# Dense edge counts for the first 512 nodes of a graph network, and how its one-hots are built

## What is computed

```python
def _sage_layer(x, src, dst, inv_deg, W_self, W_neigh, b):
    agg = jax.ops.segment_sum(x[src], dst, num_segments=N_NODES)
    mean = agg * inv_deg[:, None]
    return x @ W_self + mean @ W_neigh + b
...
x = x + gnn(layernorm(x))          # three such layers, relu between them
x = x + ffn(layernorm(x))          # gelu(x w1 + b1) w2 + b2 for the selected nodes, scaled by the weight
```

## Time and profile before

| | us |
|---|---|
| time before, median of 3 runs | 6282.49 (6279.57 to 6283.19) |
| the profiled execution | 6277.99 |
| its span | 6276.2 |
| gathers of layer 0 | 145.8 to 2101.0 |
| gathers of layer 1 | 2136.5 to 4091.8 |
| gathers of layer 2 | 4110.9 to 6089.5 |

### The profile page before, as it was taken

One profiled execution on the slowest core, in us unless ns is written; L12 is line 12 of the kernel. 1 busy time (PEld: TensorE's weight loads), 2 busy tenths in 40 slices (PEclk: granted clock), 3 DMA queues, 4 the chain that ended last, 5 costly groups with the idle time before them and its releaser, 6 DMA issues.

```text
span 6276.2 us, 96211 instructions
## 1 busy us (share of the span) xinstructions
PE 4104.0 (65%) x20011; PEld 2433.3 (39%) x20012; DVE 2259.7 (36%) x4900; ACT 946.2 (15%) x2227; POOL 4448.2 (71%) x4700
## 2 busy tenths in 40 slices
PE   0445656677778645555666676654566788899993
PEld 0222333344445322222223333322234556677772
DVE  7112223333444311122223334421223344555556
ACT  6000000111111100000000000100011223334440
POOL 0777777777777577777777777767777777777750
PEclk9677778888999866677777788866778899999996
DMA  7555555565666555555556666655555656666644
GB/s 246 158 158 160 163 165 166 168 170 170 173 174 175 148 158 158 163 164 165 167 168 170 171 173 175 176 147 159 161 164 165 168 170 170 175 175 176 178 136 167
DMA packets 459717, 1053.84 MB, mean 168 GB/s; under 512 B 127891, under 2 KB 234087, under 8 KB 459687
## 3 DMA queue, kind: packets, MB, share of 16 engines
q0 software_dynamic: 300288, 922.79, 52.5%
q10 hardware_dynamic: 82908, 97.60, 4.5%
q1 hardware_dynamic: 76491, 33.10, 2.0%
HBM read 969.11 MB, written 84.02 MB: 168 GB/s over the span
## 4 chain that ended last, share of the span: by engine, by line
POOL 47%; issue 19%; PE 19%; DMA 11%; DVE 2%; ACT 1%; POOLq 1%; DVEq 0%; SPq 0%; ACTq 0%
POOL gath L494 47%; DMA gath<-table,idx_ring 10%; PE agg L609 8%; PE agg L611 3%; PE y L664 2%; PE hid L654 2%; PE y L548 1%; DMA idx_ring<-idx_dram 1%; PE hid L548 0%; PE hid L611 0%; PE lo L611 0%; PE hid L573 0%; DMA resid<-x 0%; POOLq L490 0%; PE tp L535 0%
## 5 line engine op out<-in xcount | busy, mean ns | idle before, releaser
L494 POOL DMA_INDIRECT gath<-table,idx_ring x4692 | 4447.4, 948 | 1641.5 <-issue 1539.4
L609 PE MATMUL agg<-gath,onehot 128*128 x5856 | 2464.8, 450 | 2007.9 <-SPq L429 1815.4
L609 PEld LDWEIGHTS agg<-gath,onehot 128*128 x5856 | 633.7, 108 | 3086.4 <-issue 2776.8
L883 DVE TENSOR_TENSOR onehot<-ids_ps,dst_f 128x512 f32 x1464 | 1012.8, 692 | 1980.3 <-PE agg L611 1126.5
L611 PE MATMUL agg<-gath,onehot 128*128 x3904 | 1238.2, 317 | 0.0
L611 PEld LDWEIGHTS agg<-gath,onehot 128*128 x3904 | 424.1, 109 | 127.8
L914 DVE SCALAR_TENSOR_TENSOR resid<-agg,inv_deg,resid 128x256 f32 (+1 forms) x196 | 94.7, 483 | 863.8 <-PE agg L611 863.1
L664 PE MATMUL y<-w_sb,hidT 128*128 128x256 f32 x1568 | 378.0, 397 | 3.0 <-ACT hidT L1244 3.0
L654 PEld LDWEIGHTS hid<-featT,w_gnn 128*128 128x128 f32 x3136 | 365.9, 192 | 4.9
L654 PE MATMUL hid<-featT,w_gnn 128*128 128x128 f32 x3136 | 366.5, 275 | 0.0
L1131 ACT ACTIVATE featT<-tp 128x256 f32<-128x256 f32 x196 | 75.0, 383 | 1886.3 <-PE tp L535 1769.3
(11 more groups left out here) (136 smaller groups left out, 2750.8 us busy)
## 6 DMA issues: line engine op xcount, KB each, us to landing
gath<-table,idx_ring POOLq DMA_INDIRECT x4692
table<-split ACTq DMA_DIRECT2D x194, 192.0 KB
table<-gath ACTq DMA_DIRECT2D x24, 768.0 KB, 3.6
xb<-x ACTq DMA_DIRECT2D x97, 128.0 KB
yw_dram<-yw ACTq DMA_DIRECT2D x97, 128.0 KB, 2.9
resid<-x SPq DMA_DIRECT2D x24, 512.0 KB, 7.8
gath<-yw_dram SPq DMA_DIRECT2D x24, 512.0 KB, 8.8
out<-gath ACTq DMA_DIRECT2D x24, 512.0 KB, 9.0
```

The costliest lines, as they stand in the source:

```text
L494: g.indirect_dma_start(gath[:, j, 0:PARTS * D], None, table[layer][:, :], bass.IndirectOffsetOnAxis(ap=idx_ring[:, h, i:i + 1], axis=0)).t ...
L609: mm(agg[p][:, 0:2 * D], oh, tile_rows[:, :, 0:2 * D], start=False, **flags)
L883: v.tensor_tensor(onehot[:, bass.ds(pair, GROUP), :], window_ids[p].unsqueeze(1).to_broadcast([P, GROUP, P]), dst_f[:, bass.ds(tiles, GROU ...
```

## The change

Nodes 0 to 511 (windows 0 to 3, `DENSE`) get their sums in layers 1 and 2 from a dense matrix of edge counts, not from gathers.

- In layer 0, slots 6 to 69, the counts are built. 128 groups of four nodes, two in a slot: for each edge tile of a group VectorE writes a one-hot of the source's low seven bits (128 columns) and one of four nodes times 100 source chunks (400 columns); TensorE multiplies them into the bank `count_ps`; ScalarE copies the 400 columns to `stage`, and stores them to DRAM each eight groups. Ahead of it, in slot 4, the sources are split and the groups' tile borders are counted.
- In layers 1 and 2 the windows come in the order 4 to 34, then 0 to 3, then 35 to 97 (`window_of`). In slots 6 to 30 TensorE multiplies a block of counts (1 MB) with 512 rows of the layer's f32 features (512 KB), four chunks by four windows, and sums into two PSUM banks; ScalarE issues both loads a slot ahead. In slots 31 to 34 nothing is gathered.
- GpSimd and SyncE start both layers at the turn of window 4's first block (`t0`, counted in turns).
- ScalarE also copies each product in f32 (`y32`) and stores it for the dense part. `w2` is loaded after layer 0, since its buffer serves the counts.
- `RING` is 16 tiles, four blocks, and the index ring is halved with it. Half of the output's buffers lie in the new buffer `dense`.
- `ids_ps` is gone. In layer 1 the window's ids lie in `count_ps` and one operation writes a block's one-hots as before; in layers 0 and 2 four operations do, one for each tile, each adding the window's base to `iota_row` and comparing with the tile's destinations.

The core of the diff:

```diff
-RING = 32
+RING = 16
...
+DENSE = 4
+CHUNKS_PER_BLOCK = 4
+GROUP_NODES = 4
+COUNT_COLS = 100
+DENSE_AT = 6
+COUNT_AT = 6
+COUNT_RING = 4
...
+        y32 = [sb(f"y32_{p}", [P, D]) for p in range(2)]
+        group_tiles = sb("group_tiles", [1, COUNT_GROUPS + 1], I32)
+        skipped = sb("skipped", [1, 2], I32)
...
-        ids_ps = psum("ids_ps", [P, 512])
-        window_ids = [ids_ps[:, p * P:(p + 1) * P] for p in range(2)]
...
+        count_ps = psum("count_ps", [P, 512])
+        dense_banks = [None, (lo0[:], hid[:, 1, :]), (lo0[:], count_ps[:])]
+        dense_ps = [banks and [t[:, h * D:(h + 1) * D] for t in banks for h in range(2)] for banks in dense_banks]
+        window_ids = [count_ps[:, p * P:(p + 1) * P] for p in range(2)]
...
+        def window_of(layer, n, part):
+
+
+            if layer == 0 or not exists(n):
+                return n
+            if isinstance(n, int):
+                if n < DENSE_WINDOWS:
+                    return n + DENSE
+                return n - DENSE_WINDOWS if n < DENSE_WINDOWS + DENSE else n
+            return n + DENSE if part[0] == 0 else n
...
-            sp.dma_start(w2_sb[:], w2.rearrange("(k p) n -> p k n", p=P)).then_inc(w_loaded, 16)
...
+            sp.dma_start(src_low.bitcast(I32), idx_dram[:, 0:PADDED]).then_inc(src_loaded, 16)
...
+            pool.wait_ge(steps_ready, 1)
+            t0, turns_left = first_block(pool)
...
+                with pool.Fori(t0 if layer else 0, FULL_TURNS) as it:
...
+            def count_group(g):
+
+                lo, hi = pe_groups(g)
+                pe.wait_ge(count_copied, g + 2)
+                flags = dict(start=False, skip_group_check=True)
+                mm(count_ps[:, 0:1], zeros[:], ones_bf[:, 0:1], start=True, stop=False, skip_group_check=True)
+
+                def count_tile(t, stop):
+                    slot = pe.snap((t + g) % COUNT_RING)
+                    pe.wait_ge(count_hots, t + g + 1)
+                    return mm(count_ps[:, 0:GROUP_NODES * COUNT_COLS], low_hots[:, bass.ds(slot, 1), :],
+                              key_hots[:, bass.ds(slot, 1), :], stop=stop, **flags)
+                with pe.If(lo < hi):
+                    with pe.Fori(lo, hi) as t:
+                        count_tile(t, False).then_inc(count_used, 1)
+                count_tile(hi, True).then_inc(count_ready, 1)
...
+                for c in range(2 if last_block else CHUNKS_PER_BLOCK):
+                    r = TAIL_ROWS if last_block and c == 1 else P
+                    for w in range(DENSE):
+                        ends = last_block and c == 1
+                        last = mm(dense_ps[layer][w], counts[p][0:r, w * P:(w + 1) * P, c], node_rows[p][0:r, c, :],
+                                  start=False, stop=ends, skip_group_check=True)
+                last.then_inc(dense_done, 1)
...
+                w = window_of(layer, n, part)
+                if not gathered(layer, w):
+                    pe.wait_ge(dense_done, layer * DENSE_BLOCKS)
+                    pe.wait_ge(agg_ready, layer * NT + n)
+                    pe.sem_inc(agg_ready, 1)
+                    return
+                first, shared = pe_blocks(half_of(layer, half, part, w), p)
+                if layer and isinstance(n, int) and n == 0:
+                    first = pe.snap(pe_t0 * RING_BLOCKS)
...
+                if part and part[0] == 0:
+                    for j in range(2):
+                        count_group(part[1] * 8 + (part[2] * 2 + j))
...
+                dense_step(1, w, p, part)
...
+            RING_BITS = RING_BLOCKS.bit_length() - 1
+            v.tensor_scalar(skipped[0:1, 0:1], win_block[0:1, DENSE // 2, 0:1], RING_BITS, None,
...
-                    dve.wait_ge(slots_free, b + (layer * PADDED_BLOCKS + 2))
-                    v.tensor_tensor(onehot[:, bass.ds(pair, GROUP), :],
-                                    window_ids[p].unsqueeze(1).to_broadcast([P, GROUP, P]),
-                                    dst_f[:, bass.ds(tiles, GROUP)].unsqueeze(2).to_broadcast([P, GROUP, P]),
-                                    ALU.is_equal).then_inc(onehot_ready, 1)
+                    dve.wait_ge(slots_free, b + dve_base[layer])
+                    if layer == 1:
+                        v.tensor_tensor(onehot[:, bass.ds(pair, GROUP), :],
+                                        window_ids[p].unsqueeze(1).to_broadcast([P, GROUP, P]),
+                                        dst_f[:, bass.ds(tiles, GROUP)].unsqueeze(2).to_broadcast([P, GROUP, P]),
+                                        ALU.is_equal).then_inc(onehot_ready, 1)
+                        return
+                    dve.sem_inc(dve_turn, 1)
+                    for j in range(GROUP):
+                        last = v.tensor_scalar(onehot[:, bass.ds(pair, GROUP), :][:, j, :], iota_row[:],
+                                               window_base[:, col(w)], dst_f[:, bass.ds(tiles, GROUP)][:, j:j + 1],
+                                               ALU.add, ALU.is_equal)
+                    last.then_inc(onehot_ready, 1)
...
+                    o = feat[p] if layer < 2 else rest
+                    dve.sem_inc(half_added, 1)
+                    if layer == 1:
+                        dve.wait_ge(tp_ready, turned(2, n - 2))
+                    v.scalar_tensor_tensor(out=o[0:r, :], in0=dense_ps[layer][w][0:r, :], scalar=inv, in1=total,
+                                           op0=ALU.mult, op1=ALU.add
+                                           ).then_inc(feat_ready if layer < 2 else o_ready, 1)
+                    return
...
+            def count_onehots(g):
+
+                lo, hi = dve_groups(g)
+                dve.wait_ge(count_copied, g + 1)
+                dve.sem_inc(dve_turn, 1)
+                with dve.Fori(lo, hi + 1) as t:
+                    slot = dve.snap((t + g) % COUNT_RING)
+                    dve.wait_ge(count_used, t + 2)
+                    dve.sem_inc(dve_turn, 1)
+                    v.tensor_scalar(low_hots[:, bass.ds(slot, 1), :], iota_row[:].unsqueeze(1),
+                                    src_low[:, bass.ds(t, 1)], None, ALU.is_equal)
+                    v.tensor_scalar(key_hots[:, bass.ds(slot, 1), :], iota_keys.unsqueeze(1),
+                                    group_base[:, col(g)], src_key[:, bass.ds(t, 1)],
+                                    ALU.add, ALU.is_equal).then_inc(count_hots, 1)
...
+                y = product_ps(phase, p)[0:r, 0:D]
+                a.copy(y32[p][0:r, :], y)
+                a.copy(split[p][0:r, 0, :], y).then_inc(hi_ready, 1)
                 act.wait_ge(rest_ready, upto(phase, n))
+                act.wait_ge(hi_ready, upto(phase, n))
+                act.dma_start(window_rows(rows_f32[phase], w), y32[p][0:r, :]).then_inc(y32_stored[p], 16)
...
+                    a.copy(stage[:, :, j * GROUP_NODES:(j + 1) * GROUP_NODES, :].rearrange("p k n c -> p n k c"),
+                           count_ps[:, 0:GROUP_NODES * COUNT_COLS].rearrange(
...
+                act.dma_start(counts[p].rearrange("p n c -> p (n c)"),
+                              counts_dram[k if isinstance(k, int) else bass.ds(k, 1)].rearrange(
+                                  "l t x -> l (t x)" if isinstance(k, int) else "o l t x -> (o l) (t x)")
+                              ).then_inc(counts_loaded[p], 16)
...
+                    act.dma_start(node_rows[p], window_span(rows_f32[layer], k * CHUNKS_PER_BLOCK)
+                                  ).then_inc(node_rows_loaded[p], 16)
```

More of the change, by code:

```diff
@@ L577, in _, with count_ends @@
             pe_blocks = pair_blocks(pe)
[L579 to L581 removed]
+            def count_ends():
+                pe.wait_ge(src_split, 1)
+                sums = (TILES - 1 + 511) // 512
+                for c in range(sums):
+                    cols = min(512, TILES - 1 - c * 512)
+                    if c:
+                        pe.wait_ge(ends_done, c)
+                    mm(count_ps[:, 0:cols], ident[:, P - 1:P].to_broadcast([P, P]), dst_f[:, c * 512:c * 512 + cols],
+                       start=True, stop=True).then_inc(ends_bcast, 1)
+                pe.wait_ge(ends_done, sums + 1)
+                nc.tensor.transpose(count_ps[0:1, 0:P], ends_count, ident[:]).then_inc(group_T, 1)
```

379 lines of the change are left out of this document (293 added, 86 removed).

## The result

The changed kernel took 6461.38 us (median of 4 runs, 6459.74 to 6466.26), the kernel before beside it 6281.03: a ratio of 1.0289, with a 95% interval of 1.0271 to 1.0306. It is 2.9% slower; the forecast was 6170 and the range 5900 to 6450. The profiled execution of the changed kernel took 6462.66 us, of which its span is 6460.9.

A forecast was written before the change was run, and what follows sets the result against it. GpSimd's gather issue was taken as the bound in layers 0 and 1, TensorE only in layer 2's late windows. 6278 − 761 + 340 + 40 + 245 + 25 = 6167, or 6170 against the median; range 5900 to 6450.

The forecast's parts named there:

- What is removed: Layers 1 and 2: 304 gathers fewer in each, 608 x 1.251 = 761 us off.
- VectorE's terms in layer 0: Slots 6 to 69: fixed work, one-hot blocks, counting tiles and groups sum to 1487 us against GpSimd's 1171; VectorE becomes the bound.
- TensorE's half clock, +40: Layer 0: the first one or two blocks after each count run at 2.6 us instead of 1.3; 40 us added.
- The limit of 10 us: Ring of 16: GpSimd stops if TensorE's other work in a slot is over about 10 us.
- Layer 1, +40: Layer 1: 20 us from 25 dense slots, some 10 from slots 31 to 34, 10 from DMA; bounds 0 and 150.
- Layer 2, later windows, net 40: Layer 2 after slot 35: TensorE the bound as now, VectorE's chain up to 3 us late; 63 slots, net 40 us.
- Slots 31 to 35 of layer 2, 29: Layer 2, slots 31 to 34 and start of 35: no block freed for five times 7.7 us, costing 29 us.
- DMA: Layer 1: 1.5 MB more per slot fits under the slot but may delay landing rows; 10 us.
- The port, 10 us: Layer 2: one-hots with one SBUF tensor source beside gathers cost 10 us through the shared port, bounded at 25.
- the engine's pitch: Rival, layer 0: operations run at VectorE's own pitch, layer 0 costs about 35 us, total 5865; chance 0.24.
- TensorE at the half clock through all blocks: Rival, layer 0, slots 6 to 69: all 298 blocks at 2.6 us cost 283 us, total 6413; chance 0.24.
- The signs to look for: Trace afterwards: 4084 gathers, layer 0 about 340 us longer, VectorE almost never idle, layer 2 waits of 5 to 7 us.

The follow-up runs named there:

- a_ids_sbuf: The changed kernel with one operation per block of one-hots in every layer, ids in SBUF: 6465.13 us, ratio 1.0274.
- a_no_count: The changed kernel without counting one-hots, counting products and copies of counts: 6056.85 us, ratio 0.9632.
- all_mid: The changed kernel with counts and dense products behind the window's first blocks and one-operation one-hots in every layer: 6075.59 us, ratio 0.9682.
- b_ring16: The kernel before with a ring of 16 tiles instead of 32, nothing else changed: 6373.88 us, ratio 1.0129.
- b_ring16_up: The kernel before with a ring of 16 and layer 2's first feed-forward product behind the window's first block: 6263.62 us, ratio 0.998.
- a_dense_mid: The changed kernel with dense products behind the window's first block: 7794.3 us, in a set where the kernel before took 7852 us.

## Why the prediction was wrong

- **What is removed:** right. 608 gathers went, at 1.251 us each wherever GpSimd was free to run.
- **VectorE's terms in layer 0:** right in size. A block 1.62 us (1.65 forecast), a counting tile 1.06 (1.2), a group about 1.6 as forecast (idle times of 1.7 to 2.0 us ahead of its first operation, of which 0.3 are in any loop turn), so 298 x 1.62 + 445 x 1.06 + 128 x 1.6 + 256 = 1415 us against 1487. **The conclusion from them failed:** VectorE is not the bound by itself. a_ids_sbuf took 187 us from VectorE and nothing from the layer. The sum for one engine was compared with the sum for GpSimd, and the order was left out: both groups lie ahead of the window, so TensorE waits for VectorE's counting tiles and frees nothing meanwhile, and VectorE waits 209 us for TensorE to come to them. In part the two engines' times add where I had laid them over each other. No run deepens `COUNT_RING`, which would let VectorE count further ahead. I had the rule for it in the paragraph on the ring, and applied it to layers 1 and 2 alone. Counting cost 421 us (a_no_count) where I had 301 + 40.
- **Counting tiles spread evenly:** the groups are four nodes each and the lists are sorted, so group 0 has 28 tiles and group 1 has 13. Slot 6 alone holds 41, and the longest wait of layer 0 is 44.1 us. Windows 0 to 9 lost 103.
- **TensorE's half clock, +40:** the first products of a block after a count do run at 0.63 us where 0.38 is the full clock (the engine had waited before). Of TensorE's products `agg<-gath,onehot` in windows 6 to 69 of layer 0, 50% take over 0.5 us, where 22% did before and 23% do without the counting (a_no_count). It lengthens the piece, and no run prices it alone.
- **The limit of 10 us:** about right. In the slot of layer 2 GpSimd went on for 10.3 us after TensorE's last product of the window (4799.3 to 4809.6). But the piece is 16.0 us, not 15 (`y` 4.70 us in place of 3.65, the dense products 7.6 in place of 7.2), so windows 10 to 34 lost 8.2 us each where I had 6.6: 206 us against 165.
- **Layer 1, +40 (measured 119):** the mis-sized term is the piece, 107 us in windows 10 to 34 where I had 20. The layer product was costed at the full clock and the dense products at 7.2; measured they are 3.1 and 7.6, with the transposes 10.7 us from 3014.07 to 3024.79, and the blocks around run at 0.63 us a product too, so a slot lost 4.3 in place of 1 to 2. Window 35 lost 10, as forecast. TensorE's timeline in one dense slot of layer 1:

```profile
3014.07 3.10 PE L664 MATMUL y<-hidT,featT 128*128 128x512 f32 x4
...
3017.22 1.20 PE L738 MATMUL lo<-dense 128*128 128x256 f32 x4
...
3024.79 0.17 PE L779 MATMUL agg<-ones,zeros 128*128 128x1 bf16 x1
```

  The clock of the whole stretch (0.75 before, 0.81 after) hid that just this product runs at the half clock: the granted clock is 0.50 from 3005 to 3014, where TensorE waits for rows, 0.58 in the product's 3 us, and 1.00 in the dense products. Moving the products took 83 us back (all_mid).
- **Layer 2, later windows, net 40 (windows 40 to 97 lose 142 us, 19 before: +123):** the mechanism was named and mis-sized. "After slot 35 TensorE is the bound as now" left the ring's own price out, and VectorE's late chain was put at net 40. b_ring16 loses 114 us in these windows without any of the change, 2 us a window, with TensorE's wait of 2 us for ScalarE behind VectorE's late one-hots, as shown above; the dearer one-hots are the other 28. How much of it is VectorE's lead and how much GpSimd's full ring stays open, as one edit mends both (b_ring16_up, 109 of 116 back).
- **Slots 31 to 35 of layer 2, 29:** the longest wait there is 43.1, and window 35 lost 50.
- **DMA:** the dense loads landed in 6.5 us (1 MB) and 10.0 (512 KB), inside a slot. They cost layer 1 some 9 us by the waits for index loads, at most 19; I had 10.
- **The port, 10 us:** the gathers' mean rose from 951 to 957.6 ns in layer 2 and from 946.3 to 953.8 in layer 0, 8 + 12 us of gather time.
- **The rivals:** the engine's pitch did not hold (a block takes 1.62 us for 1.11 of work). TensorE at the half clock through all blocks did not hold either: it was about half of the products, and the granted clock is 0.77 over layer 0 where it was 0.83. It puts 243 us more than I did into layer 0, where the miss is 114, and none into layers 1 and 2, where it is 220, so that the time came out near its 6413 is luck. The slower sign came from a mechanism that I had named and under-applied, the piece.
- **The signs to look for:** 4084 gathers, GpSimd at 5 tenths and the pitch of a block came as written; a counting tile's pitch was 1.06 for 1.2, and the waits in layer 2 were near 8 us for 5 to 7. "Layer 0 about 340 us longer" (454) and "VectorE with almost no idle time" did not; VectorE idle in layer 0 was among the signs of being wrong.

## What to carry to other kernels

A sum per engine tells the bound only if the ring between two engines covers the longest piece in which the consumer gives nothing back; write down that piece for every stage, with the waits inside it and with what every other engine on the same ring must put off behind it, before halving a ring. Where it is too long, change the order first: the same work laid between the blocks, with the cheaper one-hots, turned a loss of 2.9% into a gain of 6%. And cheapen an engine only after that: the cheaper operation gave nothing alone and 105 us once the order was mended.

## What the runs showed of the hardware

One-hots with two tensor sources in SBUF lengthen the gathers beside them, but little. All gathers of the changed kernel and of a_ids_sbuf (count, busy us, mean ns):

```profile
L605 POOL DMA_INDIRECT gath<-table,idx_ring x4084 | 3891.6, 953 | 2409.9 <-issue 1365.7
```
```profile
L607 POOL DMA_INDIRECT gath<-table,idx_ring x4084 | 3970.7, 972 | 2334.5 <-issue 1363.2
```

79 us with some 900 such operations of 0.69 us, under 0.1 us for each. The gathers of layer 1, which both kernels have alike, are 3 ns longer in this run too, so some 13 of the 79 us are not the one-hots'. The Trainium skill, SBUF — State Buffer, section Who interferes with whom, says that a VectorE instruction with two inputs in SBUF contends with a GpSimd instruction that reads SBUF, and that the lock of a two-port mode, which holds for a whole instruction, is not for `tensor_tensor`; no run here shows a wait of 0.69 us as a rule, and which port a gather needs is not visible in the trace.

The kernel before took 7852 us through one whole set of runs, where it takes 6276 to 6292 otherwise. The gathers of the kernels beside it are not longer (median 946 to 949 ns, as otherwise). Part of the rest is idle time that ends in nothing the trace shows, in the middle of VectorE's loops, as here in layer 0 of a_dense_mid, where the pitch of a counting tile is 1.06 us otherwise:

```profile
2025.10 0.29 DVE L1214 TENSOR_SCALAR dense<-iota_row,dense 128x128 f32 x1 [0.53 <-issue]
2026.55 0.53 DVE L1216 TENSOR_SCALAR dense<-w_sb,dense 128x400 f32 x1 [1.16 <-issue]
2032.94 0.29 DVE L1214 TENSOR_SCALAR dense<-iota_row,dense 128x128 f32 x1 [5.87 <-issue]
```

Its cause stays open. Comparisons hold only beside a run of the kernel before in the same set.
